# State-space stage with the scan product ahead of C·B and the skip term as a diagonal matmul; routing stage with the low parts of the weights made expert by expert

## The reference

```python
# state-space block (Mamba-2), chunks of 128 tokens, 4 heads of 64 channels, state size 64
zxbcdt = x @ W_in
z, xBC, dt = jnp.split(zxbcdt, [D_INNER, D_INNER + CONV_DIM], axis=-1)
conv = conv_b + sum((xp[:, k:k + L, :] * conv_w[:, k] for k in range(D_CONV)))
xBC = jax.nn.silu(conv)
xh, Bmat, Cmat = jnp.split(xBC, [D_INNER, D_INNER + D_STATE], axis=-1)
...
Y = (Y_diag + Y_off + xh * D[:, None]).reshape(Bsz, L, D_INNER)
Y = Y * jax.nn.silu(z)
Y = Y * jax.lax.rsqrt(jnp.mean(Y * Y, axis=-1, keepdims=True) + EPS) * norm_w
out = Y @ W_out
return out @ W_lin + b_lin
```

## Time and profile before

| | |
|---|---|
| time, median of 3 runs | 1245.38 us (1243.94 to 1248.22) |
| profiled execution | 1249.54 us, its span 1247.8 us |
| PE, DVE, ACT, POOL busy | 84%, 68%, 57%, 32% of the span |
| state-space stage | from 447.5 to 766.8 us of the span |
| routing stage | from 766.8 us on |

### The profile page before, as it was taken

One profiled execution on the slowest core, in us unless ns is written; L12 is line 12 of the kernel. 1 busy time (PEld: TensorE's weight loads), 2 busy tenths in 40 slices (PEclk: granted clock), 3 DMA queues, 4 the chain that ended last, 5 costly groups with the idle time before them and its releaser, 6 DMA issues. The chain is left out here.

```text
span 1247.8 us, 23207 instructions
## 1 busy us (share of the span) xinstructions
PE 1053.5 (84%) x6746; PEld 925.6 (74%) x6746; DVE 846.9 (68%) x2117; ACT 712.4 (57%) x1560; POOL 400.6 (32%) x413
## 2 busy tenths in 40 slices
PE   2999999999995946899999975567609999899998
PEld 2988889898884924566666665566509999899997
DVE  5576767667667636999999964799854555445554
ACT  4466564655652238888888853666504555455554
POOL 4232232322314600001000001457662444524444
PEclk9999999999996567788788876788658999999999
DMA  4121212112100022123212302735234544333331
GB/s 157 60 69 44 85 42 82 44 44 82 34 1 24 1 72 62 40 68 68 64 47 60 68 1 83 233 112 160 82 128 122 150 127 126 95 96 96 99 95 56
DMA packets 82778, 99.14 MB, mean 79 GB/s; under 512 B 9483, under 2 KB 68626, under 8 KB 82554
## 3 DMA queue, kind: packets, MB, share of 16 engines
q1 hardware_dynamic: 72490, 74.31, 22.0%
q0 software_dynamic: 8752, 21.25, 4.9%
q10 hardware_dynamic: 1440, 2.40, 0.6%
HBM read 72.30 MB, written 27.02 MB: 80 GB/s over the span
## 5 line engine op out<-in xcount | busy, mean ns | idle before, releaser
L1616 PE MATMUL e_p_y<-w,e_gT 128*128 (+1 forms) x852 | 118.2, 275 | 0.0
L1563 DVE TENSOR_TENSOR e_g<-e_sl,e_p_h 128x342 f32<-128x342 f32 x142 | 72.6, 511 | 63.5 <-ACT e_sl L1541 55.5
L877 POOL TENSOR_TENSOR m_rs<-m_ms,m_minus_half 128x4 f32<-128x4 f32 x16 | 18.6, 1164 | 300.5 <-ACT m_ms L910 300.5
L1616 PEld LDWEIGHTS e_p_y<-w,e_gT 128*128 128x128 f32 (+1 forms) x852 | 106.1, 191 | 0.4 <-issue 0.4
L1545 ACT ACTIVATE e_gT<-e_p_gx 128x384 f32<-128x384 f32 x142 | 69.6, 490 | 63.9 <-PE e_p_gx L1606 63.9
L87 PE MATMUL e_p_h<-w_hi,e_xT_hi 128*128 x284 | 104.5, 368 | 1.5 <-DVE e_g L1563 0.8
L1541 ACT ACTIVATE e_sl<-e_p_h 128x342 f32<-128x342 f32 x142 | 64.8, 457 | 69.7 <-PE e_p_h L89 69.5
L1567 DVE TENSOR_TENSOR e_xT_lo<-e_p_gx,e_xT_hi 128x128 fp32r<-128x128 f32 x142 | 41.4, 292 | 86.2 <-ACT e_xT_hi L1549 85.9
L1527 POOL DMA_INDIRECT sorted_scratch<-e_xg x71 | 69.0, 972 | 91.2 <-DVE e_xg L1573 89.6
L1525 POOL DMA_INDIRECT out<-e_xg x71 | 68.9, 970 | 85.9 <-DVE e_xg L1573 79.9
L968 DVE SCALAR_TENSOR_TENSOR m_c<-m_p_x,m_vecs,m_c 128x506 f32<-128x506 f32 (+2 forms) x144 | 95.5, 735 | 0.0
(11 more groups left out here) (357 smaller groups left out, 3356.3 us busy)
## 6 DMA issues: line engine op xcount, KB each, us to landing
e_xg<-sorted_scratch SPq DMA_DIRECT2D x142, 130.0 KB, 2.1
m_cum<-cum_scratch SPq DMA_DIRECT2D x16, 1024.0 KB
g_adjT<-in_adjT SPq DMA_DIRECT2D x16, 512.0 KB, 4.0
g_adj<-in_adj SPq DMA_DIRECT2D x16, 512.0 KB
c_adjT<-in_adjT SPq DMA_DIRECT2D x16, 512.0 KB, 6.5
x_tokens<-in_x SPq DMA_DIRECT2D x16, 256.0 KB, 5.0
sorted_scratch<-nothing SPq DMA_DIRECT2D x2, 1040.0 KB, 10.1
sorted_scratch<-nothing SPq DMA_DIRECT2D x12, 130.0 KB, 2.6
```

Source lines behind the costliest of these rows:

```text
L1563: dve.tensor_tensor(g[:, i % D3], sl[:, i % 2], p_h3[i % 2][:, 0:HP], ALU.mult).then_inc(q["g_ready"], 1)
L1616: last = pe.matmul(p_y[d % 2][:, 0:P], gT[0:r, d % D3, k], w2k[:, bass.ts(e, P)], start=k == 0, stop=k == len(CH) - 1)
```

## The change

In the state-space stage:

- The scan product Y of step i-2 moves ahead of the product of C and B of step i-1 on PE; it now follows the transposes.
- The skip term moves from DVE to PE. Before the loop, DVE makes two 128×128 diagonal matrices `skip` (the identity times D). For each graph and head, PE first multiplies a 128×64 slice of `skip` with the activated x (256 columns) into the same accumulation as Y: 8 more f32 matmuls in each step. `y1` and its two DVE instructions are gone; `y2` reads PSUM directly.
- What waited for `y1_ready` now waits for `y2_ready` (z and Y on PE) or `Y_done` (ACT's silu of x).

In the routing stage the subtraction for a weight tensor is written as 8 POOL instructions of 128×341 in place of one of 128×2728.

```diff
@@ mamba_phase, scalar
-                    need(act, q["y1_ready"], 2 * (d - 2))
+                    need(act, q["Y_done"], d - 2)
@@ mamba_phase, vector
+            for k in range(2):
+                dve.tensor_scalar(skip[:, k], eye[:], D[:, k:k + 1], None, ALU.mult).then_inc(q["skip_ready"], 1)
             for i in range(END):
                 s, d, v, y, o = i, i - DEC, i - W_LAG, i - GATED, i - OUT
                 if live(y):
                     dve.wait_ge(q["Y_done"], y + 1)
-                    dve.wait_ge(q["xs_ready"], y + 1)
-                    need(dve, q["y2_ready"], y)
-                    for k in range(2):
-                        dve.scalar_tensor_tensor(out=y1[:, k], in0=xs[:, y % 3, k], scalar=D[:, k:k + 1], in1=p_zY[:, k], op0=ALU.mult, op1=ALU.add).then_inc(q["y1_ready"], 1)
-                    dve.wait_ge(q["y1_ready"], 2 * (y + 1))
                     dve.wait_ge(q["zs_ready"], y + 1)
                     need(dve, q["out_done"], y - 1)
                     need(dve, q["sq_ready"], y - 1)
-                    dve.tensor_tensor(y2[:, y % 2], y1[:], zs[:, y % 3], ALU.mult).then_inc(q["y2_ready"], 1)
+                    dve.tensor_tensor(y2[:, y % 2], p_zY[:], zs[:, y % 3], ALU.mult).then_inc(q["y2_ready"], 1)
@@ mamba_phase, tensor: z
-                    need(pe, q["y1_ready"], 2 * (s - 2))
+                    need(pe, q["y2_ready"], s - 2)
@@ mamba_phase, tensor: after the transposes, ahead of the product of C and B (which stays as it was)
+                if live(v):
+                    pe.wait_ge(q["zs_ready"], min(s + 1, STEPS))
+                    need(pe, q["y2_ready"], v)
+                    if live(o):
+                        pe.wait_ge(q["ms_ready"], o + 1)
+                    pe.wait_ge(q["W_ready"], 2 * (v + 1))
+                    pe.wait_ge(q["xdt_ready"], v + 1)
+                    pe.wait_ge(q["xs_ready"], v + 1)
+                    pe.wait_ge(q["skip_ready"], 2)
+                    for g in range(G):
+                        for h in range(HEADS):
+                            k, p0 = h // 2, h % 2 * HD
+                            hs = slice(h * HD, (h + 1) * HD)
+                            l0 = g * N
+                            pe.matmul(p_zY[p0:p0 + HD, k, l0:l0 + N], skip[:, k, p0:p0 + HD], xs[:, v % 3, k, l0:l0 + N], start=True, stop=False)
+                            pe.matmul(p_zY[p0:p0 + HD, k, l0:l0 + N], xdt[:, v % 2, 2 * g, hs], W[:, v % 2, g, h, 0:N], start=False, stop=False)
+                            last = pe.matmul(p_zY[p0:p0 + HD, k, l0 + P:l0 + N], xdt[:, v % 2, 2 * g + 1, hs], W[:, v % 2, g, h, N:NB], start=False, stop=True)
+                    last.then_inc(q["Y_done"], 1)
@@ dispatch_phase, gpsimd
-                    pool.tensor_tensor(dst.lo[:, :, 0:H], raw[n], dst.hi[:, :, 0:H].bitcast(F32), ALU.subtract).then_inc(q["w_split"], 1)
+                    for e in range(EX):
+                        pool.tensor_tensor(dst.lo[:, e, 0:H], raw[n][:, e], dst.hi[:, e, 0:H].bitcast(F32), ALU.subtract).then_inc(q["w_split"], 1)
```

More of the change, by code:

```diff
@@ L841, in mamba_phase @@
         W = sb("W", [P, 2, G, HEADS, NB])
-        y1 = sb("y1", [P, 2, S])
+        skip = sb("skip", [P, 2, P])
         y2 = sb("y2", [P, 2, 2, S])
@@ L1004, in _ @@
                     pe.wait_ge(q["zs_ready"], min(s + 1, STEPS))
-                    need(pe, q["y1_ready"], 2 * min(s - 2, STEPS))
+                    need(pe, q["y2_ready"], min(s - 2, STEPS))
                     pe.wait_ge(q["sq_ready"], o + 1)
@@ L1026, in _ @@
                     last.then_inc(q["G_done"], 1)
-                if live(v):
-                    pe.wait_ge(q["zs_ready"], min(s + 1, STEPS))
-                    need(pe, q["y1_ready"], 2 * (v - 0))
-                    if live(o):
-                        pe.wait_ge(q["ms_ready"], o + 1)
-                    pe.wait_ge(q["W_ready"], 2 * (v + 1))
-                    pe.wait_ge(q["xdt_ready"], v + 1)
-                    for g in range(G):
-                        for h in range(HEADS):
-                            k, p0 = h // 2, h % 2 * HD
-                            hs = slice(h * HD, (h + 1) * HD)
-                            l0 = g * N
-                            pe.matmul(p_zY[p0:p0 + HD, k, l0:l0 + N], xdt[:, v % 2, 2 * g, hs], W[:, v % 2, g, h, 0:N], start=True, stop=False)
-                            last = pe.matmul(p_zY[p0:p0 + HD, k, l0 + P:l0 + N], xdt[:, v % 2, 2 * g + 1, hs], W[:, v % 2, g, h, N:NB], start=False, stop=True)
-                    last.then_inc(q["Y_done"], 1)
 BF16 = mybir.dt.bfloat16
```

4 lines of the change are left out of this document (2 added, 2 removed).

## The result

| | before | after |
|---|---|---|
| median of 6 runs | 1244.44 us (1243.66 to 1248.22) | 1237.56 us (1236.78 to 1241.01) |
| ratio to before, 95% interval | | 0.9939 [0.9923, 0.9954] |
| profiled execution, its span | 1249.54, 1247.8 us | 1237.73, 1236.0 us |

The change takes 6.9 us off the median, where 3.6 were predicted. The two profiled executions differ by 11.8 us: the one of before lay 5.1 us over its median, the one of after 0.2. So the traces say where the time went, and the medians how much it was.

The account below looks back on a forecast made before the run. It took three nearly equal rings to bound the state-space stage, ACT's 16.9 us the longest given. Middle 0, fill -1.0, drain -3.5 and routing +0.9 summed to -3.6 us: 1241.8 us from a 1245.38 us median, range 1234 to 1250.

Parts of the forecast that it names:

- rival B: State-space middle: PE's clock holds and steps fall to 16.9 us, -5.6 us there, 1236.2 us in all; chance 0.20.
- The reading of what bounds the kernel: State-space stage: three rings of nearly equal length, no engine far ahead; freeing DVE by itself worth 0 in the middle.
- ACT's ring: State-space step on ACT, from one silu of x to the next: 16.9 us, a step can't fall much under it.
- The middle, 0 us: Eleven state-space steps between fill and drain: steps stay at 17.4 us, gain 0, between -5.6 and +7.5 us.
- the idle time isn't gone, it moves: about 2 us: PE in each middle step: idle time moves from before C·B to ahead of the next input products, about 2 us.
- Rival C: State-space middle: slow clock moves onto the input products, steps of 18.0 us, +3.9 us in all, 1249.3 us; chance 0.18.
- Rival E: PE's skip products of two heads don't pair: 3.4 us a step at full clock, +2.4 us in all, 1247.8 us; chance 0.10.
- Fill, -1.0 us: Start of the state-space stage: next input products start 1.4 us sooner, partly eaten by the mask's DMA; 0 to -1.4.
- Drain, -3.5 us: End of the state-space stage: Y starts right after the transposes and y2 comes 3.7 us sooner; 0 to -4.5.
- Routing, +0.9 us: Routing stage: DVE's wait for POOL stays and grows by 0.45 us in each of two places; 0 to +2.1.
- rival D: Routing: DVE gets in between POOL pieces, -1.3 us in place of +0.9, 1239.6 us, or 1232.9 if all pass freely; chance 0.12.
- the first is nearest (same operation, same stage), so the wait stays: Routing: c_vr taken to behave like c_den, which lost two queued POOL instructions, so the wait grows: +0.9 us.

Follow-up runs that it names:

- last batch: Four kernels with POOL pieces spread, Y ahead of or behind C·B, skip term on PE or on DVE with unused products: 1229.03 to 1236.49 us.
- order_only: Kernel before with only Y moved ahead of C·B on PE, skip term still on DVE, one POOL instruction per tensor: ratio 1.0029.
- skip_first: Changed kernel with Y back behind C·B, four skip products of 512 columns between transposes and C·B, POOL pieces spread over two iterations: 1229.03 us, ratio 0.9867.
- hole_filled: Kernel before plus eight skip products between transposes and C·B, overwritten by Y, skip term still on DVE: ratio 0.9933, -8.3 us.
- order_dummy: Kernel before with Y ahead of C·B and eight skip products that are overwritten, y1 still on DVE, one POOL instruction per tensor: ratio 0.9985.
- pieces_only: Kernel before with only the routing subtraction split into eight POOL pieces per tensor: ratio 0.9971, -3.7 us.

## Why the prediction was right, and where not

The direction and the range held (1241.8 us, 1234 to 1250; measured 1237.56). Two of the four terms of the sum had the wrong mechanism: the middle was put at 0 and routing at a loss, and both gained. That the time still lay inside is owed to the range, which took in rival B, and in this the forecast had luck.

- **The reading of what bounds the kernel** held. ACT's ring was given as 16.9 us, and undisturbed steps take 16.80. That no gain would come from DVE by itself in the middle held too: its freed time became the wait at L949, 15.6 us. Over the whole stage the relief was worth more than the sum had for it, 3.4 to 4.2 us (last batch), and where it lies is open.
- **The middle, 0 us: wrong, it was rival B** (-5.6 us; the two profiled executions -5.1, the means of all traces -4.4). The step that failed is "the idle time isn't gone, it moves: about 2 us". It was worked out as 16.9 less 14.8 us of PE work; measured are 0.74 us. Three terms were short: from the taps' end to the transposes' end 9.6 us (662.54 to 672.14) instead of 9.15, 0.37 of it a wait ahead of the squares' products; Y with the skip 4.96 us (655.27 to 660.23) instead of 4.3; C·B 1.57 us (660.23 to 661.80) instead of 1.3. Together 1.4 us, two thirds of the hole. PE's idle time was a small difference of large terms. The comparison "2 us isn't much shorter than 2.81" rested on the longest hole of the trace; the usual one was 1.32 us. And "both the hole and the thing that follows it persist" came true in order_only, with 2.90 us in each step (18.27 us a step), not in the changed kernel with 0.74.
- **Rival C**, the slow clock on the input products, didn't come, but its mechanism and its price did in order_only: 18.27 us a step, forecast 18.0. The condition for it was put wrongly. It isn't that Y with the skip uses up the slack: the stretch at 0.50 shown above lies on Y and the skip, and cost 0.2 us. In order_only it is the empty hole ahead of the input products that does it.
- **Rival E** didn't come: the skip records of two heads overlap. Standing alone, skip_first's four products of 512 columns take 1.94 us and hole_filled's eight of 256 1.95, where 4 × 0.43 = 1.7 was predicted for pairs and twice that for unpaired ones.
- **Fill, -1.0 us**: measured -2.1, beyond its bound of -1.4. It lies in the third step, 16.8 us before and 14.5 after: the wait for the first Y went as said (1.51 us), and `y1` (1.41 us) with it. But `y1`'s part is given back, DVE then waits 0.63 and 3.06 us for the DMA of the decay exponents, and order_dummy with `y1` still on DVE has a fill of 64.6 us. Nor does it take the earlier Y: hole_filled, with Y behind C·B, doesn't wait for the first Y either and has a fill of 63.9. The clock from 490 to 508 us is 1.00 there, 0.91 after and 0.78 before; that the filled hole speeds the fill too was missing from the term. **Drain, -3.5 us**: measured -2.5 in this pair of traces and -3.3 in the means, so the size was right. Y and y2 came sooner as worked out, but the squares' products ahead of the transposes fell to the low clock, and the wait for the transposes grew by 2.4 us.
- **Routing, +0.9 us: wrong sign, it was rival D** (-1.3 us; traces -1.4, pieces_only -3.7 with -5.7 to -1.8). The step that failed is "the first is nearest (same operation, same stage), so the wait stays". The choice between two rows was made by likeness of the DVE instruction. D's -1.3 us fits these traces, but not the -3.7 of pieces_only; what else gained there is open. The rows of after show both behaviours again, `c_den` losing two queued POOL instructions and `c_vr` to `c_shift` one piece each. The Trainium skill, "SBUF — State Buffer", section "Who interferes with whom", has a DVE instruction with two SBUF inputs and a GpSimd instruction that reads SBUF contend for a shared port pair that is "an exclusive lock". The eight pieces agree with it (0.83 us for a piece of 0.87), `c_den` at 830.18 (1.84 us over two) doesn't. What makes the difference wasn't tried.

What stays open: where in the stage `y1` on DVE and the move of Y cost their 3 to 7 us, since traces of the same code differ by as much; and whether the clock hangs on the length of a hole or on what stands around it.

## What to carry to other kernels

When PE falls to the low clock in each step of a loop, look for the hole just ahead of the fall and move work into it before anything else. The largest part of this gain came from 2 us of products put where PE had been idle for 1.3 us in most steps, useful or not, and skip products on the other side of the hole made the kernel 2% slower. Moving the hole doesn't help if an engine that bounds the loop waits for what comes behind it; price an order by which instructions the low clock will lie on.

Work out the hole that a change leaves to a few tenths, from an unbroken chain of rows. It is the difference of large terms: 2 us were predicted, 0.74 came. And read the hole of before over all steps, not from one: the step that was looked at had 2.81 us, nine of eleven had 1.32.

When a change is made of several edits, run them in all pairings. Here one edit of three was a loss of 3 to 7 us that the sum hid, and undoing it (skip_first) gave the fastest kernel.

On POOL, long work beside a chain of small DVE instructions belongs in short pieces, and best around the chain instead of under it: pieces at the same place gave 1.4 us in the traces (2.5 in the five iterations on the other chip), two ahead of the chain and two behind it another 4.2 to 4.7.

## What was unexpected of the hardware

- Work whose result is overwritten made the kernel faster: eight products of 256 columns in each step, -8.3 us (-10.6 to -6.0).
- A DVE instruction of 8 elements a partition can lose 0.83 us to one POOL piece of 0.87 and be let in before the next, four times in a row, and elsewhere lose two queued POOL instructions (1.84 us) in one go.
- 24 products in which the two heads alternate three shapes (skip, Y, Y) overlap less well than the same columns apart: 4.96 us together, where the skip products take 1.95 us alone and Y 2.8 us alone (order_only, 647.75 to 650.55). That is 0.2 us, but of a hole of 0.74.
